# Softmax denominators by a matmul with zeros and ones in a planned single-core kernel

## What is computed

```python
q, k, v = shape(h @ Wq.T), shape(h @ Wk.T), shape(h @ Wv.T)
scores = einsum('bhqd,bhkd->bhqk', q, k) * SCALING + position_bias
attn = softmax(scores, axis=-1)
ctx = einsum('bhqk,bhkd->bhqd', attn, v).transpose(0, 2, 1, 3).reshape(b, s, D_MODEL)
...
topw, topi = top_k(softmax(xf @ w_router), 2); topw = topw / sum(topw)
g = silu(einsum('td,xdh->txh', xf, wg)); u = einsum('td,xdh->txh', xf, wu)
out = einsum('txd,tx->td', einsum('txh,xhd->txd', g * u, wd), combine)
```

## Time and profile before

| | |
|---|---|
| median of 3 runs | 988.42 us (985.24 to 991.22) |
| profiled execution | 983.89 us, its span 982.1 us |
| mean granted TensorE clock | 0.953 |
| TensorE (PE) busy | 846.8 us, 86% |
| VectorE (DVE) busy | 641.8 us, 65% |
| ScalarE (ACT) busy | 557.4 us, 57% |
| GpSimd (POOL) busy | 299.0 us, 30% |

### The profile page before, as it was taken

The page is one execution under the profiler, slowest core; times in us unless marked ns, Lnnn a source line. Parts: engine busy times, 40 slices in busy tenths (PEclk is TensorE's granted clock), DMA queues, the critical chain, the costliest instruction groups (busy, mean ns, idle before and its releaser), DMA issues.

```text
span 982.1 us, 36375 instructions
## 1 busy us (share of the span) xinstructions
PE 846.8 (86%) x15235; PEld 514.6 (52%) x15235; DVE 641.8 (65%) x1566; ACT 557.4 (57%) x974; POOL 299.0 (30%) x387
## 2 busy tenths in 40 slices
PE   5888989889889988979887899798899789879895
PEld 3334435545444544545444545456465566757793
DVE  2547585976677566657767866568485566656773
ACT  3556747666485836745756566454558364425552
POOL 2432222222331322132223202325223343443452
PEclk9999999999799999979999899999999899989998
DMA  7998100000000000000000100001100011114633
GB/s 178 388 333 296 49 24 8 8 24 8 29 18 14 12 14 19 9 23 3 19 22 15 36 18 19 23 19 32 42 19 19 28 46 40 50 44 126 178 104 123
DMA packets 50190, 60.90 MB, mean 62 GB/s; under 512 B 5872, under 2 KB 36464, under 8 KB 49648
## 3 DMA queue, kind: packets, MB, share of 16 engines
q1 hardware_dynamic: 34768, 27.19, 9.6%
q10 hardware_dynamic: 10272, 21.14, 6.3%
q0 software_dynamic: 4992, 10.27, 3.1%
HBM read 22.92 MB, written 35.65 MB: 60 GB/s over the span
## 4 chain that ended last, share of the span: by engine, by line
PE 48%; DVE 27%; issue 11%; ACT 5%; POOL 4%; DMA 3%; another core or an unknown queue 1%; SPq 0%; POOLq 0%; DVEq 0%; ACTq 0%
DVE row_max L1336 13%; PE ps L927 9%; PE ps L787 6%; PE ps L754 5%; PE ps L1012 4%; PE ps L765 3%; POOL eo_rows L1640 2%; PE ps L801 2%; PE ps L810 2%; PE ps L1004 2%; PE ps L793 2%; PE ps L1006 2%; PE ps L1005 2%; ACT probs L1164 2%
## 5 line engine op out<-in xcount | busy, mean ns | idle before, releaser
L1336 DVE TENSOR_REDUCE row_max<-ps 128x4 f32<-128x1024 f32 (+1 forms) x256 | 267.7, 1078 | 109.6 <-PE ps L765 62.7
L1164 ACT ACTIVATE probs<-ps 128x1024 f32<-128x1024 f32 x128 | 130.1, 1029 | 77.8 <-PE ps L787 66.7
L754 PE MATMUL ps<-bias_t,ch 64*32 64x512 f16 x2048 | 112.1, 395 | 26.7 <-DVE row_max L1336 12.2
L1164 ACT ACTIVATE stage<-ps 128x1024 f32<-128x1024 f32 x96 | 96.9, 1025 | 60.1 <-remote 31.7
L1640 POOL DMA_INDIRECT eo_rows<-eo_t,to_t x92 | 89.4, 972 | 117.8 <-ACT eo_t L1216 97.0
L1604 POOL TENSOR_TENSOR ctx_sb<-ctx_raw,ctx_sb 128x512 f32<-128x512 f32 x32 | 40.7, 1272 | 172.6 <-DVE ctx_sb L1364 172.5
L927 PE MATMUL ps<-probs,v_pad 128*32 128x256 f32 x1024 | 85.4, 400 | 3.2 <-ACT probs L1164 2.0
L1004 PE MATMUL ps<-xT_t,wgu_hi 128*128 128x256 f16 x276 | 77.6, 281 | 8.8 <-issue 2.8
L1495 DVE SCALAR_TENSOR_TENSOR gate_s<-gate_t,ps 128x256 f32<-128x256 f32 x138 | 57.1, 414 | 40.5 <-ACT gate_t L1210 30.8
L1627 POOL DMA_INDIRECT slot_rows<-rows,slots x64 | 63.2, 987 | 66.1 <-DVE slots L1444 51.8
L1012 PE MATMUL ps<-wd,hid 128*128 x552 | 74.2, 287 | 9.9 <-ACT xT_t L1202 5.8
(11 more groups left out here) (168 smaller groups left out, 1596.1 us busy)
## 6 DMA issues: line engine op xcount, KB each, us to landing
slot_rows<-eo_g ACTq DMA_DIRECT2D x1, 12642.0 KB, 48.0
slot_rows<-eo_g ACTq DMA_DIRECT2D x1, 7998.0 KB, 26.1
x_t<-slot_rows SPq DMA_DIRECT2D x46, 129.0 KB
eo_g<-eo_rows SPq DMA_DIRECT2D x16, 256.0 KB
xT<-in_x SPq DMA_DIRECT2D x16, 128.0 KB
kept<-resid SPq DMA_DIRECT2D x16, 128.0 KB, 1.7
resid_b<-kept SPq DMA_DIRECT2D x16, 128.0 KB
out_dram<-outT SPq DMA_DIRECT2D x16, 128.0 KB
```

The costliest lines, as they stand in the source:

```text
L754: eng.matmul(ps[HR * c:HR * (c + 1), two[r], :].rearrange("p (j s) -> p j s", j=2), csth("flip")[half, :], bias_t[half, way, 2 * g:2 * g + ...
L1164: eng.activation(probs[a][:, 2 * (k % 2):2 * (k % 2) + 2, :], both_of("c%d" % a, i, "e%d" % k), ACT.Exp).then_inc(z["exp"], 1)
L1336: ins = eng.tensor_reduce(row_max[a][:, qt, 4 * g:4 * g + 4].rearrange("p (r j) -> p r j", r=2), of_heads, AX.X, ALU.max)
```

## The change

The two transposes and the small reciprocal go. In their place a matmul `den` with a constant 128x128 matrix of zeros and ones spreads each denominator over the rows of its head: row `m` of the result is the denominator for row `m`. One reciprocal of 128x512 reads it from PSUM and writes `ctx_sb`; GpSimd's product follows as before. In job `h` ScalarE and VectorE write only the first copy of the rows, GpSimd makes the second copy and the targets (`pool_twice`), and GpSimd also makes the residual (`pool_resid`), in two instructions in place of VectorE's one. The plan's entries change with it, and the constants grow by 128 columns.

```diff
     def back(self, a, i, free):
         last = self.op((job, i, "ctx"), "act", 0.60, ...)
-        last = self.chain(job, i, last, ("byq", "dve", 0.62), ("rec", "dve", 0.35), ("byd", "dve", 0.62), ("ctxn", "pool", 1.3))
+        last = self.chain(job, i, last, ("den", "pe", 0.85, ONE), ("rec", "dve", 0.69, (), "mine"), ("ctxn", "pool", 1.3))
...
     def b1(self, i):
-        last = self.back(1, i, [("h", i - 3, "comb")] if i > 2 else [])
+        last = self.back(1, i, [("h", i - 3, "resid")] if i > 2 else [])
...
     def b2(self, i):
-        last = self.back(2, i, [("h", i - 1, "comb")] if i else [])
+        last = self.back(2, i, [("h", i - 1, "resid")] if i else [])
...
     def h(self, i):
-        last = self.op(("h", i, "top"), "dve", 1.9, [last], (), "mine")
+        last = self.op(("h", i, "top"), "dve", 1.5, [last], (), "mine")
+        twice = self.op(("h", i, "twice"), "pool", 0.9, [last])
-        self.op(("h", i, "comb"), "dve", 1.1, [("h", i, "gap")])
-        self.op(("h", i, "kept"), "sp", 0.4, [("h", i, "comb")])
+        self.op(("h", i, "comb"), "dve", 0.5, [("h", i, "gap")])
+        self.op(("h", i, "resid"), "pool", 1.4, [("b2", i, "end")])
+        self.op(("h", i, "kept"), "sp", 0.4, [("h", i, "resid")])
...
-            last = self.op(("h", i, "scatter%d" % q), "pool", 1.2, [last] + ...)
+            last = self.op(("h", i, "scatter%d" % q), "pool", 1.2, [last, twice] + ...)
...
         def pe_back(eng, a, i, at):
+            yield at("den")
+            bank = free_bank(eng, job, i, "den")
+            if a == 1 and i == 0:
+                eng.wait_ge(s_w2, 16 * N_W2)
+            eng.wait_ge(z["ctx"], i + 1)
+            eng.matmul(bank, cst("den"), ctx_raw[a][:, :, :].rearrange("p r s -> p (r s)"), start=True, stop=True).then_inc(z["den"], 1)
             yield at("out")
             bank = free_bank(eng, job, i, "out")
-            if a == 1 and i == 0:
-                eng.wait_ge(s_w2, 16 * N_W2)
...
-            eng.activation(rows[:, i % 2, :, :, 0:D], tokens_twice(i), ACT.Copy).then_inc(hand["hi"], 1)
+            eng.activation(rows[:, i % 2, 0, :, 0:D], tokens(i), ACT.Copy).then_inc(hand["hi"], 1)
...
         def dve_back(eng, a, i, at):
-            yield at("byq")
-            eng.wait_ge(z["ctx"], i + 1)
+            yield at("rec")
+            eng.wait_ge(z["den"], i + 1)
             if i:
                 eng.wait_ge(z["o"], i)
-            flat = ctx_sb[a][:, :, :].rearrange("p r s -> p (r s)")
-            eng.transpose(flat, ctx_raw[a][:, :, :].rearrange("p r s -> p (r s)")).then_inc(z["byq"], 1)
-            yield at("rec")
-            eng.wait_ge(z["byq"], i + 1)
-            eng.reciprocal(rden[a][:, :, 0:2], flat.rearrange("p (n m) -> p n m", m=HR)[:, :, 16:18]).then_inc(z["rec"], 1)
-            yield at("byd")
-            eng.wait_ge(z["rec"], i + 1)
-            eng.transpose(flat.rearrange("p (n d) -> p n d", d=HD),
-                          rden[a][:, :, :].rearrange("p n k -> p (n k)").unsqueeze(2).to_broadcast([P, 4 * KT * S // HR, HD])) \
-               .then_inc(z["byd"], 1)
+            eng.reciprocal(ctx_sb[a][:, :, :], held(job, i, "den").rearrange("p (r s) -> p r s", r=2)).then_inc(z["rec"], 1)
...
         def dve_h(eng, i):
-            eng.tensor_tensor(rows[:, i % 2, :, :, D:2 * D], tokens_twice(i), rows[:, i % 2, :, :, 0:D], ALU.subtract) \
+            eng.tensor_tensor(rows[:, i % 2, 0, :, D:2 * D], tokens(i), rows[:, i % 2, 0, :, 0:D], ALU.subtract) \
                .then_inc(hand["lo"], 1)
-            eng.tensor_scalar(rows[:, i % 2, :, :, 2 * D:2 * D + 2].bitcast(F32), cst("to").rearrange("p (k t c) -> p k t c", k=2, c=1),
-                              float(2 * i * S), None, ALU.add).then_inc(hand["to"], 1)
...
-            if i >= 2:
-                eng.wait_ge(s_keep[i % 2], 16 * (i // 2))
-            eng.scalar_tensor_tensor(out=resid[:, i % 2, :], in0=h2T[:, :], scalar=modT[:, i, GB:GB + 1],
-                                     in1=x1T[:, i % 3, :], op0=ALU.mult, op1=ALU.add).then_inc(hand["resid"], 1)
...
+        def pool_resid(eng, i):
+            yield PLACE["h", i, "resid"]
+            eng.wait_ge(h2_done, i + 1)
+            if i >= 2:
+                eng.wait_ge(s_keep[i % 2], 16 * (i // 2))
+            eng.tensor_scalar(resid[:, i % 2, :], h2T[:, :], modT[:, i, GB:GB + 1], None, ALU.mult).then_inc(hand["resid"], 1)
+            eng.wait_ge(hand["resid"], 2 * i + 1)
+            eng.tensor_tensor(resid[:, i % 2, :], resid[:, i % 2, :], x1T[:, i % 3, :], ALU.add).then_inc(hand["resid"], 1)
+
+        def pool_twice(eng, i):
+
+            yield PLACE["h", i, "twice"]
+            eng.wait_ge(hand["lo"], i + 1)
+            both_k = rows[:, i % 2, :, :, :]
+            eng.tensor_copy(both_k[:, 1, :, 0:2 * D].bitcast(F32), both_k[:, 0, :, 0:2 * D].bitcast(F32)).then_inc(hand["twice"], 1)
+            eng.tensor_scalar(both_k[:, :, :, 2 * D:2 * D + 2].bitcast(F32), cst("to").rearrange("p (k t c) -> p k t c", k=2, c=1),
+                              float(2 * i * S), None, ALU.add).then_inc(hand["twice"], 1)
...
+    den = np.zeros((P, P))
+    for m in range(P):
+        den[m // HR * HR + 2 * HD + (1 if HD <= m % HR < 2 * HD else 0), m] = 1.0
+    put("den", den)
```

More of the change, by code:

```diff
@@ L43 @@
 for _n, _w in (("ident", P), ("centre", D), ("kmask", HJ), ("kones", HJ), ("expert", NX), ("tri", NX * NX), ("tile", T_MAX), ("eights", T_MAX),
-               ("first", len(PARTS) * NX), ("zero", 1), ("half", 1), ("own", 2), ("to", 2 * KT), ("cos", KT * HD), ("sin", KT * HD)):
+               ("first", len(PARTS) * NX), ("zero", 1), ("half", 1), ("own", 2), ("to", 2 * KT), ("cos", KT * HD), ("sin", KT * HD), ("den", P)):
     CF[_n] = (CF_COLS, CF_COLS + _w)
@@ L228, in h @@
         for q in range(2 * KT):
-            last = self.op(("h", i, "scatter%d" % q), "pool", 1.2, [last] + ([("h", i - 1, "scatter3")] if i and not q else []))
+            last = self.op(("h", i, "scatter%d" % q), "pool", 1.2, [last, twice] + ([("h", i - 1, "scatter3")] if i and not q else []))
         self.op(("h", i, "end"), None, 2.0, [last])
@@ L632, in block_kernel @@
         att = {a: signals("a%d_" % a, "qk v hi again vz lo kspread qspread krow qrow score max "
-                          "mxhi mxlo maxt clear qmax wscore exp pv ctx byq rec byd ctxn o") for a in (1, 2)}
+                          "mxhi mxlo maxt clear qmax wscore exp pv ctx den rec ctxn o") for a in (1, 2)}
         x1_done, h2_done = sem("x1_done"), sem("h2_done")
         rot_done = signals("rot_", "cos sin sum")
-        hand = signals("hand_", "tok hi lo to l step gap e hot both ahead rank slot resid")
+        hand = signals("hand_", "tok hi lo twice l step gap e hot both ahead rank slot resid")
         moe = signals("moe_", "tr to xt gu tanh silu hid dn eo acc fin out plan sched")
@@ L686, in given_back @@
                 return (x1_done if job == "b1" else h2_done), i + 1
+            if name == "den":
+                return z["rec"], i + 1
             if name in ("centre", "turn"):
@@ L705, in held, with tokens @@
             return ps[:, BANK_OF[key], :]
-        def tokens_twice(i):
-            tok = held("h", i, "tok")[:, 0:S].rearrange("p (t d) -> p t d", t=KT)
-            return tok.unsqueeze(1).to_broadcast([P, 2, KT, D])
+        def tokens(i):
+            return held("h", i, "tok")[:, 0:S].rearrange("p (t d) -> p t d", t=KT)
         def pe_setup(eng):
@@ L1374, in dve_b1 @@
             if i > 2:
-                eng.wait_ge(hand["resid"], i - 2)
+                eng.wait_ge(hand["resid"], 2 * (i - 2))
             eng.scalar_tensor_tensor(out=x1T[:, i % 3, :], in0=held("b1", i, "out")[:, 0:S], scalar=modT[:, i, GA:GA + 1],
@@ L1385, in dve_b2 @@
             eng.wait_ge(norm["n2"]["h"], i + 1)
+            if i:
+                eng.wait_ge(hand["resid"], 2 * i)
             eng.tensor_tensor(h2T[:, :], hbT[:, i % 2, :], held("b2", i, "out")[:, 0:S], ALU.add).then_inc(h2_done, 1)
@@ L1445, in dve_h @@
                               ALU.max).then_inc(hand["slot"], 1)
-            eng.wait_ge(hand["resid"], i + 1)
             eng.wait_ge(st, n + 9)
@@ L1549, in pool_setup @@
             eng.memset(ones_h[:, :], 1.0)
-            for a in (1, 2):
-                eng.memset(rden[a][:, :, :], 0.0)
             eng.memset(blank, 0.0).then_inc(su["filled"], 1)
@@ L1622, in pool_h @@
                         eng.wait_ge(hand["slot"], i + 1)
-                        eng.wait_ge(hand["lo"], i + 1)
-                        eng.wait_ge(hand["to"], i + 1)
+                        eng.wait_ge(hand["twice"], 2 * (i + 1))
                         if i == PARTS[part_of[i]][0]:
@@ L1686, in sp_kept @@
             yield PLACE["h", i, "kept"]
-            eng.wait_ge(hand["resid"], i + 1)
+            eng.wait_ge(hand["resid"], 2 * (i + 1))
             eng.dma_start(kept[i], resid[:, i % 2, :]).then_inc(s_keep[i % 2], 16)
@@ L1768, in _ @@
             pool_setup(eng)
```

(2 more changed lines are left out.)

5 lines of the change are left out of this document (2 added, 3 removed).

## The result

The changed kernel takes 1059.55 us (median of 4 runs, 1056.19 to 1062.32) against 986.93 us for the kernel before in the same comparison: a ratio of 1.073, 95% interval 1.068 to 1.078. The profiled execution has 1056.2 us and a span of 1054.4. The forecast was 1037 us in a range from 992 to 1082, slower with 81 in 100. The direction and the range hold; the step is half as large again as the sum had it (+73 against +49 us).

A forecast was written before the change was run, and what follows sets the result against it. TensorE was taken to set the pace, seldom kept waiting. Late context +44, products +17, banks and queue +5, GpSimd +2, plan -18, shorter last item -1 gave +49 us: 1033 profiled, 1037 median, range 992 to 1082.

The forecast's parts named there:

- the sum: All terms added for the whole kernel: +49 us, giving 1033 us for the profiled execution and 1037 for the median.
- The reciprocal's length: VectorE's reciprocal of 128x512 from PSUM: 3.1 us by element, with 87 in 100, against the plan's 0.69.
- Rival 1: VectorE's reciprocal is short, 0.69 us, so no late context: 985 us, between 970 and 1000; chance 0.10.
- The rule of the Trainium skill: VectorE's reciprocal as an iterative divide, repeat count 8, taken as eight cycles an element: 4.3 us for 512.
- The late context: TensorE's projection waits for GpSimd's multiplication, 2.4 us late, over 32 margins: +44 us, bounds 0 and 77.
- Banks and queue behind the reciprocal: PSUM banks held longer by each product, and row maxima queued behind VectorE's reciprocal: 5 us, between 0 and 25.
- Worth of VectorE's time: A microsecond of VectorE is worth about 0.41, from 27% of the chain for 65% of the span.
- give-back: The plan sees VectorE 45 us lighter by its own entries, worth -18 us, bounds 0 and 45.
- The product with zeros and ones: 32 added f32 matmuls on TensorE, 34 us busy, half in open time or replacing fillers: +17 us.
- GpSimd's new work: Some 2 us an item on GpSimd, 32 in all, hidden; contention with VectorE +2 us, within 0 to 5.
- rival 3: Lateness adds up as idle TensorE loses its clock, 3% more at the low clock: 1080 to 1110 us; chance 0.03.
- What would show it: Profile signs: 3.1 us reciprocal, VectorE +23 us, TensorE +20, many multiplication waits, more row-maximum waits, fewer fillers than 133.

The follow-up runs named there:

- e1: The changed kernel with a copy of 128x512 in place of the reciprocal, so without the division: 970.20 us, ratio 0.985 to the kernel before.
- e12: Repeat of the copy kernel (e1) with five GpSimd memsets ahead of each multiplication, context late and VectorE free: 946.02 us, ratio 1.042 to the kernel before.
- e5: The copy kernel (e1) plus an unread 437-column reciprocal behind each copy, VectorE occupied and context in time: 963.40 us, ratio 1.062 to the kernel before.
- e11: Repeat of e5, the copy kernel with an unread 437-column reciprocal behind each copy: 962.32 us, ratio 1.059 to the kernel before.
- e4: The kernel before with the hand-over part alone (second copies, targets and residual on GpSimd), division as before: 963.81 us, ratio 0.980.
- e3: The kernel before with the new division alone (product and reciprocal of 128x512), job h as it was: 1080.59 us, ratio 1.097.
- e8: The kernel before with only the residual moved to GpSimd, and the plan's entries for it: 894.88 us, ratio 0.986.
- e2: The changed kernel with the plan told true durations, 3.35 us for the reciprocal and 1.06 for the product: 1017.60 us, ratio 1.034 to the kernel before.

## Why the prediction was right, and where it was short

*The reciprocal's length: right.* It hung on reading 0.339 us at 32 elements and 0.166 at 2 as a price by element: 5.77 ns, 3.1 us. Measured: 3.35 us, and (3350 - 1746) / 256 = 6.27 ns an element. It was put in the plan at 0.69. From 32 to 256 elements the price is (1746 - 339) / 224 = 6.28 as well; only the step from 2 to 32, the one that I had, is cheaper, and no run shows why. Rival 1 is out, and e1 shows what it would have given: 970 us, where I worked out 985.

*The rule of the Trainium skill* ("VectorE: DVE Perf Modes", "First, the fixed hardware budget"), read as eight cycles an element, gave an estimate of 4.3 us; the runs give 6.27 ns, which at the 0.96 GHz of that page is 6.0 cycles. Slow by element it is; eight it is not.

*The late context: right as a mechanism, and in size where it stands alone.* 44 us forecast from 32 margins, 42.8 us of waits measured in e12. That they meet so closely is partly luck: the margins were those of the kernel before, and those in e1's trace, whose plan is the new one, give 38 us for a delay of 2.58 us. In the changed kernel the wait shows as 15.9 us, not 44. For the reason see the next step.

*Banks and queue behind the reciprocal: the step that failed.* I had put 5 us, "the weakest of the terms", with 25 as its bound. In the changed kernel TensorE waits 29.8 us more than in e1 for the reciprocal's end, which is when a bank comes free, and 16.1 us more for lines 1349 and 1277 in VectorE's queue. That is 46 us against 15 for the late context, since TensorE, already held up, arrives at the projection later. e5 and e11, without longer held banks, price the occupied VectorE alone at 53 to 70 us. All together are 85 to 89 us where the sum had 44 + 5 = 49. I had read the margins of one reader only, the projection. Every VectorE step that TensorE needs has its own margin, and so has every bank; what is queued behind a 3.35 us instruction is late whoever ordered it. The term also named the row maxima. TensorE's waits for them grow where VectorE alone is occupied (38.3 us in e11, 16.5 in e1), but not in the changed kernel.

*Worth of VectorE's time: too low.* The factor 0.41 (27% of the chain over 65% of the span) made 20 us of the hand-over worth 8, and GpSimd's part took 2 of it back. e4 and the pair e3 and changed kernel give 21 us both times, a factor of 1 for the hand-over as a whole (e8 has 13 us for 7.6, so it is no fixed price). The give-back of 18 us in the sum was too small by this; e1 against the kernel before (-15 us, where +17 +2 -18 -1 gave 0) shows it again. These gains are why the total missed by 24 us only: +89 and -15 against +49 and 0. Two errors of opposite sign met there, and that is luck; the term for the delay by itself was short by 36 to 40 us.

*The product with zeros and ones: about right.* +17 us for the products less some 12 of the plan's give-back was +5 for the division without its length; measured +6. The chain of the group (line 941 in e1) is 35.7 us busy for 32, close to 34.

*GpSimd's new work: hidden, as said, but dearer.* The scaling of the residual by a column takes 0.943 us, above my 0.4 to 0.75; the addition 0.728, the copy 0.420, the targets 0.240: 2.3 us an item, not 2. No cost of it shows: e4 gains 21 us for 20 us less on VectorE. Lines of VectorE that are stretched beside GpSimd are more (line 1349 averages 0.579 us instead of 0.432), but in e1 as well, and 0.647 in e3, which has nothing of the new work. It comes from the new order, with the multiplication released just as VectorE starts its next step.

*The clock: a part of rival 3 came true.* It stood at 3 in 100 as a case of its own with 1080 us and more. It is a part of the loss at 1060: 0.934 against 0.967 in e1, and 30 of the 85 us of the span. The fillers went from 133 to 80 in both, so their number doesn't explain it. TensorE's 55 us more of idle time do go with it, and e2, with 162 fillers and planned gaps, has 0.963.

*What would show it:* reciprocal, busy VectorE (+56 us, where I said 23: the reciprocals are 8 us longer than I took them, lines 1349 and 1277 are stretched by 9 beside GpSimd, and the short steps that went had overlapped their neighbours, so they free less than their sum), fewer fillers and TensorE's busy time (+40 where I said 20) came. "Many pieces" at the multiplication were only 8, and more row-maximum waits did not come: they fell from 29.2 us in 37 pieces to 17.2 in 28.

## What to carry to other kernels

In a planned order, a busy share of 65% is no slack: a step 2.7 us longer than its entry cost its whole length (85 to 89 us for 85), and 42 of the 89 came back for two true numbers in the plan. When an instruction grows, look up the margin of every step queued behind it on its engine and of whoever waits for the PSUM bank it holds, and not of its own reader alone. Take reciprocals on the compact side of a spread; the hand-over part, which only shortens VectorE's queue, is the version that beats both kernels (963.8 us, ratio 0.980, 0.974 to 0.985).

## What the runs showed of the hardware

- VectorE's reciprocal costs 6.2 to 6.3 ns an element from 32 elements up: 0.166 us for 2, 0.339 for 32, 1.746 for 256, 2.877 for 437, 3.350 for 512, from PSUM and from SBUF alike. A copy of 512 from PSUM takes 0.683 us.
- GpSimd's multiplication of 128x256 by a column takes 0.943 us, longer than its addition of two tensors of that size (0.728 us), and its copy 0.420 us.
- VectorE's line 1349, with two inputs in SBUF, takes 0.30 us alone, 1.37 us beside GpSimd's multiplication of 1.26 us, and 5.98 us beside a GpSimd instruction of 5.99 us.
- The same kernel took 985 to 987 us on two chips and 908 us on two others, with VectorE's row maxima at 1.21 to 1.22 us in the traces of both kinds. The granted TensorE clock explains a part only: 0.945 to 0.957 for the kernel before on the slower chips and 0.970 to 0.977 on the faster. In the traces the slower chips also have remote waits (74 us in the kernel before) and short pauses of TensorE, which the faster chips' traces lack or hardly have. What is behind them is open.
